# Gate and mask products in tile groups; values formed beside q and k and reordered by DMA through a scratch

## The reference

```python
q = rope((x @ Wq.T + bq), 16 heads of 32)      # k the same way; v without the rotation
qk = einsum('bshd,bstd->bsht', q, k) / sqrt(D) # attention over the 16 heads of ONE token
att = softmax(qk); out = einsum('bsht,bstd->bshd', att, v)
x1 = norm(x + (out, heads and tokens swapped) @ Wo.T + bo)
# cross step: gates from [x1, ctx, ctx], 16 heads
ig = [x1,ctx,ctx] @ Wi + bi ; log_f = log_sigmoid([x1,ctx,ctx] @ Wf + bf)
D = exp(causal(cumsum(log_f)) + ig - running max); C = (x1 . ctx) * D ; h = C @ ctx / normalizer
x2 = norm(x1 + head_norm(h)); y = norm(expert_step(x2))
```

## Time and profile before

| What | us |
|---|---|
| median of three runs | 1801.04 (1797.04 to 1804.22) |
| the profiled execution, whole | 1799.05 |
| its span | 1797.6 |
| PE busy | 1604.6 (89% of the span) |
| DVE busy | 1351.9 (75%) |
| POOL busy | 918.3 (51%) |
| ACT busy | 860.0 (48%) |
| mean granted TensorE clock, share of full | 0.979 |

### The profile page before, as it was taken

The page is one execution under the profiler, slowest core; times in us unless marked ns, Lnnn a source line. Parts: engine busy times, 40 slices in busy tenths (PEclk is TensorE's granted clock), DMA queues, the critical chain, the costliest instruction groups (busy, mean ns, idle before and its releaser), DMA issues.

```text
span 1797.6 us, 67819 instructions
## 1 busy us (share of the span) xinstructions
PE 1604.6 (89%) x27618; PEld 1283.2 (71%) x27618; DVE 1351.9 (75%) x3323; ACT 860.0 (48%) x2449; POOL 918.3 (51%) x1234
## 2 busy tenths in 40 slices
PE   0788999899999999999999999999999999999974
PEld 0566777677777777777777777777777777777752
DVE  4456787777887778787878878787878788787875
ACT  2144454454554455455545544554555455445542
POOL 1033554555564565456455545654564565456553
PEclk9899999999999999999999999999999999999995
DMA  4022222222222221222222222222222222222110
GB/s 147 30 78 73 67 76 93 72 70 94 70 78 86 81 83 71 93 70 83 81 94 70 77 87 73 90 71 94 70 81 83 91 73 77 87 71 89 68 66 30
DMA packets 53829, 141.14 MB, mean 79 GB/s; under 512 B 8767, under 2 KB 10431, under 8 KB 45578
## 3 DMA queue, kind: packets, MB, share of 16 engines
q1 hardware_dynamic: 53770, 140.31, 23.1%
HBM read 122.98 MB, written 17.30 MB: 78 GB/s over the span
## 4 chain that ended last, share of the span: by engine, by line
PE 48%; ACT 17%; POOL 15%; issue 11%; DVE 8%; SPq 1%; DMA 0%; POOLq 0%; ACTq 0%; DVEq 0%
ACT Dx L640 11%; POOL Dx L752 6%; PE bank L351 5%; PE quad L421 5%; PE bank L359 4%; PE bank L360 4%; PE bank L362 4%; PE quad L408 4%; POOL xr L743 4%; PE bank L478 4%; PE bank L502 3%; PE bank L488 3%; PE bank L447 3%; PE bank L449 3%; DVE x L942 3%
## 5 line engine op out<-in xcount | busy, mean ns | idle before, releaser
L747 POOL TENSOR_TENSOR ex<-ex,w_rec 128x512 f32<-128x512 f32 x64 | 67.1, 1048 | 677.2 <-DVE w_rec L906 677.2
L640 ACT ACTIVATE Dx<-Mb,a_col 128x128 f32<-128x128 f32 x1024 | 311.8, 392 | 3.5 <-DMA Mb<-m_rows 3.5
L767 POOL TENSOR_TENSOR h_rs<-h_ve,half_neg 128x16 f32<-128x16 f32 x64 | 187.7, 2933 | 57.9 <-DVE h_ve L979 57.9
L610 ACT ACTIVATE x1T<-bank 128x512 f32<-128x512 f32 x64 | 38.3, 598 | 335.1 <-PE bank L351 335.1
L752 POOL TENSOR_SCALAR_AFFINE_SELECT Dx<-Dx 128x512 f32<-128x512 f32 x256 | 159.3, 634 | 2.2 <-ACT Dx L640 2.2
L961 DVE SCALAR_TENSOR_TENSOR Dx<-quad,Dx 128x512 f32<-128x512 f32 x256 | 156.5, 666 | 3.9 <-PE quad L466 3.3
L781 POOL TENSOR_TENSOR rs<-ve,half_neg 128x1 f32<-128x1 f32 x192 | 104.5, 544 | 51.2 <-DVE ve L927 51.2
L942 DVE TENSOR_SCALAR x<-r,mv,rs 128x512 f32<-128x512 f32 x64 | 53.7, 838 | 98.5 <-POOL rs L781 98.5
L359 PE MATMUL bank<-wq_high,x_high 128*128 128x512 f32 x256 | 116.9, 457 | 0.0
L359 PE MATMUL bank<-wv_high,x_high 128*128 128x512 f32 x256 | 113.1, 442 | 1.0 <-issue 0.9
L359 PE MATMUL bank<-wk_high,x_high 128*128 128x512 f32 x256 | 113.3, 443 | 0.0
(11 more groups left out here) (163 smaller groups left out, 4546.9 us busy)
## 6 DMA issues: line engine op xcount, KB each, us to landing
Mb<-m_rows SPq DMA_DIRECT2D x64, 1024.0 KB, 4.6
xb<-in_x SPq DMA_DIRECT2D x256, 64.0 KB
xr<-in_x SPq DMA_DIRECT2D x64, 256.0 KB, 4.1
cb<-in_ctx SPq DMA_DIRECT2D x64, 256.0 KB, 2.6
out_dram<-yo SPq DMA_DIRECT2D x64, 256.0 KB, 4.0
Dx<-in_wq SPq DMA_DIRECT2D x4, 256.0 KB, 4.7
Dx<-in_wk SPq DMA_DIRECT2D x4, 256.0 KB, 5.5
Mb<-in_wv SPq DMA_DIRECT2D x4, 256.0 KB, 5.9
```

What stands on the lines that cost most here:

```text
L640: last = go(Dx[t.parity()][:, j, n, :], Mb[t.parity()][:, h, :], ACT.Exp, bias=a_col[t.parity()][:, h:h + 1], scale=-1.0)
L767: tt(h_rs[:], h_ve[:], half_neg[:], ALU.pow).then_inc(s.hrs_sb, 1)
```

## The change

Five things change together.

1. The gate products: those of x1 and of the context (with the context's means, formerly 16 further columns) no longer add up in one PSUM region of 80 rows. They go to two regions of 48 rows of bank 7, with tile positions (0, 0) and (0, 64), and alternate. ACT copies the first with its bias, and a new DVE instruction, `m_gsum`, adds the second.
2. The mask product, one matmul of 33 rows for each of four banks, becomes four matmuls of 32 rows, each in its own row group.
3. The values: `p_v` moves from between `m_HT(d)` and `m_H(d)`, one tile late, to right behind `p_q(a)`, and goes to bank 7. ACT copies them to SBUF (`p_v`, a new place behind the last `Dx` group), SP stores them to a scratch in DRAM, and loads them back reordered (256 KB, in runs of 32 numbers, 128 bytes). `p_VT`, `p_VG` and the ACT copy of `VG` go.
4. `m_H` writes beside the scores, columns 128 to 259 of the four banks of `quad`, and so waits for `a_sub(b)`; ACT copies it with one instruction in place of two.
5. POOL takes the residual sum later in its step. The warm-up loop of PE has 62 matmuls in place of 26.

```diff
-WARM = 26
+WARM = 62
@@ SP
+            def store_v(t):
+                sp.wait_ge(s.v_sb, upto(t))
+                sp.dma_start(v_dram[t.parity()], v_sb[:]).then_inc(s.v_out, 16)
+
+            def load_VG(t):
+                sp.wait_ge(s.v_out, stored(t.older(-1)))
+                sp.wait_ge(s.O_ps, upto(t, 1))
+                source = v_dram[t.parity()].rearrange("(u m) (h d) -> (m h) u d", m=8, d=D)
+                sp.dma_start(VG[:].rearrange("p w c d -> p (w c) d"), source).then_inc(s.v_in[t.parity()], 16)
@@ PE
             def p_v(t):
-                pe.wait_ge(s.fn1_sb, upto(t, 4))
...
-                bias(4, 2)
-                product(4, x_high, x_low, 2, False).then_inc(s.v_ps, 1)
+                pe.wait_ge(s.acol_sb, upto(t, 2))
...
+                bias(7, 2)
+                product(7, x_high, x_low, 2, False).then_inc(s.v_ps, 1)
...
                 for w in range(4):
-                    mm(quad[:, w, 0:P], pair_l[:], pair_r[:], start=True, stop=True, skip_group_check=True)
+                    rows = slice(32 * w, 32 * w + 32)
+                    mm(quad[:, w, 0:P], pair_l[rows, :], pair_r[rows, :], start=True, stop=True, skip_group_check=True)
...
             def a_O(t):
...
-                pe.wait_ge(s.VG_sb, upto(t))
+                pe.wait_ge(s.v_in[t.parity()], landed(t, 1))
...
             def m_gate(t):
+                pe.wait_ge(s.v_sb, upto(t, -1))
                 pe.wait_ge(s.x1T_sb, upto(t))
...
                 for n in range(CH):
-                    mm(bank[7][0:GM, 0:P], wg_sb[:, 0, n, :], x1T[t.parity()][:, n, :], start=(n == 0), stop=False)
-                for n in range(CH):
-                    last = mm(bank[7][0:GM, 0:P], wg_ctx[:, n, :], cT[t.parity()][:, n, :], start=False,
-                              stop=(n == CH - 1))
+                    mm(bank[7][0:GW, 0:P], wg_sb[:, 0, n, :], x1T[t.parity()][:, n, :], start=(n == 0),
+                       stop=(n == CH - 1), skip_group_check=True, tile_position=(0, 0))
+                    last = mm(bank[7][64:64 + GW, 0:P], wg_ctx[:, n, :], cT[t.parity()][:, n, :], start=(n == 0),
+                              stop=(n == CH - 1), skip_group_check=True, tile_position=(0, 64))
...
             def m_H(t):
                 pe.wait_ge(s.HT_sb, upto(t))
-                pe.wait_ge(s.LT_sb, upto(t, 3))
+                pe.wait_ge(s.sub_sb, upto(t, -2))
...
-                    last = mm(bank[6 + n // 2][:, (n % 2) * TW:(n % 2 + 1) * TW], HT[:, n, :], head_t[:],
-                              start=True, stop=True)
+                    last = mm(quad[:, n, P:P + TW], HT[:, n, :], head_t[:], start=True, stop=True, skip_group_check=True)
@@ PE step
-                if b.real():
-                    p_v(b)
...
-                if b.real():
-                    p_VG(b)
...
                 if a.real():
                     p_q(a)
+                    p_v(a)
@@ DVE
+            def m_gsum(t):
+                dve.wait_ge(s.gs_sb, upto(t))
+                tt(gs[:], bank[7][64:64 + GW, 0:P], gs[:], ALU.add).then_inc(s.gsum_sb, 1)
@@ DVE step
                 if b.real():
-                    p_VT(b)
                     a_PT(b)
...
                 if e.real():
                     x_shift(e)
+                if b.real():
+                    m_gsum(b)
```

More of the change, by code:

```diff
@@ L55 @@
 LAGS = 6
-PADS = 6
+PADS = 5
 PEEL = 10
-WARM = 26
+WARM = 62
 class Tile:
@@ L171, in bass_decoder @@
         Mb = [sb(f"Mb{i}", [P, H, P]) for i in range(2)]
-        a_col = [sb(f"a_col{i}", [P, GM]) for i in range(2)]
+        a_col = [sb(f"a_col{i}", [P, GW]) for i in range(2)]
         eFM = [sb(f"eFM{i}", [P, H]) for i in range(2)]
         Dx = [sb(f"Dx{i}", [P, 4, CH, P]) for i in range(2)]
+        v_dram = nc.dram_tensor("v_rows", (2, P, E), F32, kind="Internal").ap()
         m_dram = nc.dram_tensor("m_rows", (2, H, P), F32, kind="Internal").ap()
@@ L238, in bass_decoder @@
         four = "Dx_sb Dm_sb C_sb".split()
-        two = "x_in c_in r_in mb_in".split()
-        semaphores = {n: sem(n) for n in once + each + ["y_out", "m_out"]}
+        two = "x_in c_in r_in mb_in v_in".split()
+        semaphores = {n: sem(n) for n in once + each + ["y_out", "m_out", "v_out"]}
         semaphores |= {n: [sem(f"{n}{j}") for j in range(4)] for n in four}
@@ L278, in steps @@
                 dma = {(n, k): eng.snap(u * (16 * n) + 16 * n * k) for n in (1, 4) for k in range(-1, 2)}
-                dma |= {("out", k): eng.snap(u * 32 + 16 * k) for k in range(-LAGS, 2)}
+                dma |= {("out", k): eng.snap(u * 32 + 16 * k) for k in range(-LAGS, 3)}
                 for k in range(2):
@@ L414, in a_O @@
                 pe.wait_ge(s.PT_sb, upto(t))
-                pe.wait_ge(s.VG_sb, upto(t))
-                edge(pe, t, (s.sub_sb, 0), *[(s.C_sb[j], 2) for j in range(4)])
+                pe.wait_ge(s.v_in[t.parity()], landed(t, 1))
+                edge(pe, t, (s.Hs_sb, 3), (s.sub_sb, 0), *[(s.C_sb[j], 2) for j in range(4)])
                 for v in range(4):
@@ L420, in a_O @@
                             rows = slice(32 * c, 32 * c + 32)
-                            last = mm(quad[32 * w:32 * w + 32, c, 32 * v:32 * v + 32], VG[rows, v, 32 * w:32 * w + 32],
+                            last = mm(quad[32 * w:32 * w + 32, c, 32 * v:32 * v + 32], VG[rows, w, v, :],
                                       PT[rows, w, v, :], start=True, stop=True, skip_group_check=True,
@@ L579, in p_xT, with p_v @@
                 go(chunks(x_high), bank[5][:], ACT.Copy).then_inc(s.xhigh_sb, 1)
-            def p_VG(t):
-                act.wait_ge(s.VG_ps, upto(t))
-                edge(act, t, (s.O_ps, 1))
-                go(chunks(VG), bank[4][:], ACT.Copy).then_inc(s.VG_sb, 1)
+            def p_v(t):
+                act.wait_ge(s.v_ps, upto(t))
+                if t.regs is not None or t.k >= 1:
+                    act.wait_ge(s.v_out, stored(t))
+                go(v_sb[:], bank[7][:], ACT.Copy).then_inc(s.v_sb, 1)
             def a_exp(t):
@@ L646, in m_Hs @@
                 edge(act, t, (s.hn1_sb, 1), (s.y1_sb, 1))
-                for m in range(2):
-                    last = go(Hs[:, 2 * m:2 * m + 2, :], bank[6 + m][:, 0:2 * TW].rearrange("p (c n) -> p c n", n=TW),
-                              ACT.Copy)
-                last.then_inc(s.Hs_sb, 1)
+                go(Hs[:], quad[:, :, P:P + TW], ACT.Copy).then_inc(s.Hs_sb, 1)
             def r_abs(t):
@@ L720, in step @@
                     m_Dx(c, 3)
+                if a.real():
+                    p_v(a)
                 if g.real():
@@ L863, in _, with turn @@
             red = nc.vector.tensor_reduce
-            def turn(dst, b):
-                return nc.vector.transpose(dst[:].rearrange("p (g h n) -> p h g n", h=H, n=2), bank[b][:])
+            def turn(dst, b, order):
+                return nc.vector.transpose(dst[:].rearrange(order + " -> p h g n", h=H, n=2), bank[b][:])
             def p_QT(t):
@@ L1064, in _, with pairs @@
             dve.wait_ge(s.center_set, 4)
-            for n in range(2):
-                row = slice(32 * n, 32 * n + 1)
-                nc.vector.memset(pair_l[row, :].rearrange("p (g n) -> p g n", n=2)[:, :, n], 1.0).then_inc(s.center_set, 1)
-                last = nc.vector.memset(pair_r[row, :].rearrange("p (g n) -> p g n", n=2)[:, :, 1 - n], -1e30)
-                last.then_inc(s.center_set, 1)
+            def pairs(t, rows, n):
+                if t is pair_l:
+                    return t[rows, :].rearrange("p (g h n) -> p g h n", h=H, n=2)[:, :, :, n]
+                return t[rows, :].rearrange("p (g n h) -> p g n h", h=H, n=2)[:, :, n, :]
+            nc.vector.memset(pairs(pair_l, slice(0, P), 1), 1.0).then_inc(s.center_set, 1)
+            nc.vector.memset(pairs(pair_r, slice(0, P), 0), -1e30).then_inc(s.center_set, 1)
+            dve.wait_ge(s.center_set, 6)
+            for w in range(4):
+                row = slice(32 * w, 32 * w + 1)
+                nc.vector.memset(pairs(pair_l, row, 0), 1.0)
+                nc.vector.memset(pairs(pair_l, row, 1), 0.0)
+                nc.vector.memset(pairs(pair_r, row, 0), 0.0)
+                last = nc.vector.memset(pairs(pair_r, row, 1), -1e30)
+            last.then_inc(s.center_set, 2)
             for i in range(4):
```

93 lines of the change are left out of this document (43 added, 50 removed).

## The result

| | before | after |
|---|---|---|
| median of 4 runs | 1800.52 us (1797.04 to 1804.22) | 1919.55 us (1917.38 to 1927.53) |
| ratio, 95% interval | | 1.0669 [1.0631, 1.0707] |
| profiled execution, span | 1797.6 us | 1919.2 us |
| mean granted clock of TensorE | 0.979 | 0.935 |

The account below looks back on a forecast made before the run. The prediction took a chain of waits across engines, nearly equal to PE's own time, as the bound: 1799.05 + 97.6 (steps) + 3.7 (warm-up) + 5 (scratch) + 61 (clock) = 1966 us, 1968 as median, range 1885 to 2040.

Parts of the forecast that it names:

- The ring: Chain across engines from one x1 transpose to the next: 27.64 us against 26.04, +1.60 in each of 61 steps.
- gates: Gate products on PE in two column groups: 1.02 us in place of 1.84, saving 0.82.
- gates' end to scans' end: From the gates over ACT and DVE to the scans: 3.20 us becomes 3.52, with 0.32 for m_gsum.
- q to the next x1 transposes: PE from q on: 10.95 us less the 0.41 wait plus 3.00 for the value product, 13.54.
- The two idle stretches of PE: In each step PE waits some 2.5 us ahead of m_H and about 1.5 us ahead of q.
- Scratch: Store and load of the values: hidden in the loop, 0 to 10 us in the first steps, taken as 5.
- Warm-up: 36 more warm-up products on PE ahead of the first step: 3.7 us.
- The clock: PE's idle stretches lower its clock in most steps: 1.0 us on average, 61 us in all, bounds 0 and 120.
- The case with the clock held: Rival: no clock falls in PE's steps, the longer step stays: 1907 us, chance 0.30.
- the groups do run side by side: Rival held they don't: gate products stay at 1.84 us, +50 us, 1957 or 2018 us, chance 0.05.
- The scratch is in time: Rival held the load of values comes 2 us late at a_O: about 2029 us, chance 0.06.
- The fast case: Rival: PE's own work is the bound and each step loses 1.68 us: 1706 us, 1708 as median, chance 0.08.

Follow-up runs that it names:

- e2: The kernel after without the 12 matmuls of the value product, only its bias left: 1756.11 us, 0.9749 of the kernel before.
- e3: The kernel before without the 12 matmuls of the value product, only its bias left: 1784.32 us, 0.9922 of the kernel before.
- e7: The kernel after with the two gate sums one after the other, without column groups: 2023.06 us, 1.1215 of the kernel before.
- e8: The kernel after with DVE's scans moved behind maximum and subtraction: 1976.96 us, 1.0962 of the kernel before.
- e12: The kernel after with H products back in banks 6 and 7, two ACT copies, and 12 warm-up products fewer: 1926.95 us, 1.0712 of the kernel before.
- e5: The kernel after without store and load of the values, a constant read instead: 1920.61 us, 1.0664 of the kernel before.
- e9: The kernel after with the old value path, the old layout of k and 42 warm-up products fewer: 1726.73 us, 0.9583 of the kernel before.
- e10: The kernel after with two unused fp32 matmuls ahead of m_H and 36 warm-up products fewer: 1918.35 us, 1.0652 of the kernel before.
- e4: The kernel after with H products back in banks 6 and 7 and two ACT copies: 1995.36 us, 1.1086 of the kernel before.
- e11: The kernel after with 80 warm-up matmuls instead of 62, nothing else: 2068.06 us, 1.1457 of the kernel before.
- e1: The kernel after with the old value path but the new order of k: 2075.78 us, 1.1523 of the kernel before.
- e6: The kernel after with nine unused bf16 matmuls ahead of m_H: 2078.26 us, 1.1531 of the kernel before.

## Why the prediction was right, step by step

The forecast was slower, 1968 us in a range of 1885 to 2040; it came out at 1919.55. The ring of the prediction against the step shown above:

| piece | predicted, us | measured, us |
|---|---|---|
| x1 transposes to gates | 1.53 | 829.17 - 827.54 = 1.63 |
| gates | 1.02 | 830.24 - 829.17 = 1.07 |
| gates' end to scans' end | 3.52 | 833.71 - 830.24 = 3.47 |
| to the subtraction's end | 1.63 | 835.34 - 833.71 = 1.63 |
| to q | 6.40 | 841.78 - 835.34 = 6.44 |
| q to the next x1 transposes | 13.54 | 855.22 - 841.78 = 13.44 |
| ring | 27.64 | 27.68 |

*Ring.* Right in each piece to 0.1 us. (The prediction calls its 1.02 for the gates 20% above the half of 1.84; 1.02 against 0.92 is 11%. The measured 1.07 is 16%.) e2 shows the value product on it and e3 shows it off the old one; e7 confirms the gates' 0.82 with 0.85; e8 shows that the ring runs through the scans to q; e12 that `m_H` is beside it. The two idle stretches of PE, predicted at 2.5 and 1.5 us, are 2.38 and 1.52. `m_gsum` waits for ACT, not for DVE's queue, so its 0.29 was the right price.

*Scratch.* Hidden, as said (3.5 + 3.2 us to land). e5 gives nothing for it in the first steps either, so the 5 us there were too much.

*Warm-up.* q starts at 55.98 us in the first step before and at 57.80 after: 1.8 us for 36 products, not 3.7. What these two terms gave too much, the first steps took back: the first x1 comes 7.8 us later and the first eight steps take 11.8 us more, 19.7 together against 9.6 (six steps of 1.60), 3.7 and 5. In them the clock is low: 0.53 from 76 to 84 us, where the kernel before had 1.00.

*The clock: the term of the sum that was mis-sized.* The spans differ by 121.6 us. Less 97.6, 3.7 and 5, some 15 are left for the clock; the prediction had 61. Counted from the steps themselves, the falls cost 0.4 us per step (28.01 less 27.60), 25 us over 61 steps; the kernel before has 0.1 per step of its own (26.15 less 26.05), so the difference is some 19. The largest single fall was sized rightly. Here is one in the kernel after, on PE:

```profile
753.28 1.28 PE L432 MATMUL quad<-PT,VG 32*32 32x32 f32 x128 [0.24 <-issue]
756.01 0.98 PE L373 MATMUL bank<-wq_high,x_high 128*128 128x512 f32 x1 [1.45 <-DVE x_low L886]
```

and the stretches of that q product, and of the q product in the step shown above:

```profile
756.00:760.00 4.00, 3.99 (x10) 3.13 (x12) 3.76 (x11) 2.72 (x10) 3.75 (x4) 0.58 0.00 0
...
842.00:846.00 4.00, 4.00 (x18) 3.08 (x18) 3.76 (x12) 2.43 (x9) 3.67 (x5) 1.00 0.00 0
```

After an idle stretch of 1.45 us q ran at 1.2 GHz and the step took 29.08 us, 1.5 more than at full clock, as the earlier trace rows had let me expect. After an idle stretch of 1.52 it ran at 2.4 GHz. What was sized wrongly is the step "I expect a fall in most steps ... I take 1.0 on average". Most steps do lose something, 28 of 50 (22 take 27.70 us or less), but only 3 lose the whole of about 1.5 (28.99, 29.08 and 29.14 us), and the mean is 0.4 in place of 1.0. Where a fall lies ahead of q, PE's own wait takes up a part of it, which the prediction did not count against it:

```profile
721.78 2.07 PE L501 MATMUL quad<-head_t,HT 128*128 128x132 f32 x8 [2.41 <-DVE ex L897]
...
728.49 0.58 PE L373 MATMUL bank<-wq_high,x_high 128*128 128x512 f32 x1 [0.67 <-DVE x_low L886]
```

Here `m_H` takes 2.07 us in place of 1.14, the wait ahead of q is 0.67 in place of 1.5, and the step takes 28.10 us, 0.5 more than at full clock.

I had three idle stretches of the kernel before to go by, two of them with a fall, and took two of three for the rate. The case with the clock held gave 1907; the truth lies 13 us from it and 48 from my likeliest. So the direction and the ring were foreseen, but the likeliest number is near only as far as a range of 155 us allows.

The rivals: the groups do run side by side (starts 0.01 us apart, 1.07 us in all in place of 1.84). The scratch is in time. The fast case, PE's own work as the bound, is what e9 is, 1727 us (the rival had 1708), 4.2% under the kernel before; the change doesn't reach it, since it takes PE's cover out of the softmax chain in the same edit.

## What to carry to other kernels

Before a product is moved, ask what its engine would do in the place that it leaves: a product that runs while a chain of small operations on other engines ends was almost free here (16 us in e3), and the same product behind that chain was almost fully paid for (163 us in e2). A saving in the same edit can't be read from the total: the gates and the mask in groups save 0.75 us per step in e9, and the gates alone 0.85 on the ring of the kernel after (e7), but the 3.0 us of the value product outweigh them. And when a variant is slow beyond every theory, compare the count on the instruction queue first: where the loop of an engine lies in its program can cost more than the edit under test.

## What the runs showed of the hardware

- **The place of a loop in the program.** 42 fetches of 4.54 MB / 277 = 16.4 KB are what PE's program (some 10,900 instructions) takes once: 10,900 / 256 = 42.6, with the block named below. Its two-step loop is about 1,750 instructions (the 19,887 matmuls and weight loads in 600 us of the earlier trace rows are 1,726 in two steps of 26.04). The kernels that kept its start close to that of the kernel before (e9, e10, e12, and after itself) fetched 42 times; moved on by 18 instructions (e4) 123 times, by 36 (e11) 186 times, with stops of up to 4.7 us and over 140 us more, and further still (e1, e6) 277 times. What decides how often a loop is fetched, these runs do not settle. The Trainium skill (Runtime: NRT & Kernel Launch, "Instruction fetch mechanics") has blocks of 16 KiB or 256 instructions, room for 2048 instructions on PE, and a fetch where a taken branch leaves the window. The size of a fetch and the effect agree. Its remark that only two such blocks are held does not fit PE: a loop of nearly seven blocks ran all its passes with no fetch of its own.
- **Small runs in a DMA.** 133,000 more packets under 512 B cost no time here: the load of 256 KB in 128-byte runs lands in 3.2 us, the plain store of the same size in 3.5.
- **The clock at nearly the same idle time.** In the kernel after, 1.45 us idle ahead of q and a fall, 1.52 and none. The length of that idle stretch alone does not decide; what else does, stays open. The idle stretch before it has a part: with the filler ahead of `m_H` (e10) 8 of 50 steps lose time to a fall in place of 28, and the mean clock is 0.966 in place of 0.935.
